# Third decoder layer's cross attention with the keys on the partitions

## The reference

```python
q = x @ Wq                       # [B, 128, 1024]
k, v = jnp.split(context @ Wkv, 2, axis=-1)
sim = einsum('bhid,bhjd->bhij', q, k) * 64 ** (-0.5)
sim = jnp.where(mask, sim, -finfo.max)
sim = jnp.clip(sim, -5.0, 5.0)
attn = jax.nn.softmax(sim, axis=-1)
out = einsum('bhij,bhjd->bhid', attn, v)
return out @ Wo + bo
```

## Time and profile before

| | |
|---|---|
| median of three runs | 2144.5 us |
| profiled execution, span | 2139.6 us |
| PE busy | 1891.7 us, 88% |
| DVE busy | 1520.1 us, 71% |
| ACT busy | 1370.0 us, 64% |
| POOL busy | 827.2 us, 39% |

### The profile page before, as it was taken

One profiled execution on the slowest core, in us unless ns is written; L12 is line 12 of the kernel. 1 busy time (PEld: TensorE's weight loads), 2 busy tenths in 40 slices (PEclk: granted clock), 3 DMA queues, 4 the chain that ended last, 5 costly groups with the idle time before them and its releaser, 6 DMA issues. The chain is left out here.

```text
span 2139.6 us, 40133 instructions
## 1 busy us (share of the span) xinstructions
PE 1891.7 (88%) x13875; PEld 1361.0 (64%) x13945; DVE 1520.1 (71%) x4153; ACT 1370.0 (64%) x5428; POOL 827.2 (39%) x951
## 2 busy tenths in 40 slices
PE   6998989889998998998888999615899996899998
PEld 5757944535786965874444688404467775467776
DVE  4676788788655666779789855695876664786665
ACT  3686589827654587668963765343677774567666
POOL 2461056615432354025643533111543333543334
PEclk9999999979999999999998999867999998999999
DMA  5000000000001000000000000300000000000000
GB/s 228 1 1 1 2 1 1 1 1 2 1 2 34 1 2 1 1 2 1 1 1 1 1 2 1 111 0 13 1 2 1 1 1 24 1 1 1 1 1 11
DMA packets 6980, 24.79 MB, mean 12 GB/s; under 512 B 752, under 2 KB 3440, under 8 KB 6128
## 3 DMA queue, kind: packets, MB, share of 16 engines
q1 hardware_dynamic: 6768, 22.09, 2.8%
HBM read 21.04 MB, written 1.05 MB: 10 GB/s over the span
## 5 line engine op out<-in xcount | busy, mean ns | idle before, releaser
L1358 POOL TENSOR_TENSOR a_probs<-a_probs,a_rinv 128x512 f32<-128x512 f32 x352 | 367.3, 1044 | 421.9 <-DVE a_rinv L1191 417.5
L997 ACT ACTIVATE a_probs<-score_bank,a_negmax 128x128 f32<-128x128 f32 x896 | 315.7, 370 | 64.5 <-DVE a_negmax L1171 62.8
L1358 POOL TENSOR_TENSOR c_probs<-c_probs,c_rinv 128x512 f32<-128x512 f32 x192 | 201.1, 1047 | 296.2 <-DVE c_rinv L1191 294.2
L836 PEld LDWEIGHTS second_bank<-const,a_probs 128*128 128x128 f32 x1408 | 167.4, 142 | 193.4 <-DVE a_probs_t L1198 101.4
L803 PE MATMUL score_bank<-a_km,a_qg 128*128 128x512 f32 x512 | 267.6, 604 | 2.6 <-issue 0.9
L836 PE MATMUL second_bank<-const,a_probs 128*128 128x128 f32 x1408 | 218.4, 278 | 40.8 <-DVE a_probs_t L1198 32.8
L1366 POOL TENSOR_TENSOR a_rstd<-a_ve,neg_half 128x1 f32<-128x1 f32 x128 | 70.5, 551 | 357.6 <-DVE a_ve L1249 356.2
L1171 DVE TENSOR_REDUCE a_negmax<-score_bank 128x4 f32<-128x512 f32 x224 | 154.0, 687 | 67.7 <-PE score_bank L803 53.0
L997 ACT ACTIVATION_READ_ACCUMULATOR a_probs<-score_bank,a_negmax 128x1 f32 x896 | 188.2, 210 | 0.0
L1198 DVE COPY a_probs_t<-second_bank 128x512 f32<-128x512 f32 x272 | 179.6, 660 | 3.9 <-PE second_bank L836 3.9
L1021 ACT ACTIVATE c_probs_t<-second_bank 128x512 f32<-128x512 f32 x160 | 95.3, 595 | 109.9 <-PE second_bank L836 109.5
(11 more groups left out here) (308 smaller groups left out, 4590.3 us busy)
## 6 DMA issues: line engine op xcount, KB each, us to landing
w_L_ffn<-in_L_ffn SPq DMA_DIRECT2D x1, 3184.0 KB, 14.4
w_L_xattn<-in_L_xattn SPq DMA_DIRECT2D x1, 2112.0 KB, 24.2
w_L_xattn<-in_L_xattn SPq DMA_DIRECT2D x1, 2050.0 KB, 10.3
a_xt<-in_xT SPq DMA_DIRECT2D x3, 512.0 KB, 3.6
a_x<-in_x SPq DMA_DIRECT2D x3, 512.0 KB, 3.7
a_ct<-in_ctxT SPq DMA_DIRECT2D x3, 512.0 KB, 5.8
w_L_attn<-in_L_attn SPq DMA_DIRECT2D x1, 1345.5 KB, 17.2
w_L_attn<-in_L_attn SPq DMA_DIRECT2D x1, 1157.0 KB, 5.8
```

Of the source, the lines that this page charges most:

```text
L836: mm = pe.transpose(bank[:, j * S:(j + 1) * S], Pb[:, n % 4, j * S:(j + 1) * S], ident)
L997: op = act.activation(p, score_bank[n % 3][:, j * width:(j + 1) * width], ACT.Exp, bias=negmax[:, n % 4, j:j + 1], accum_out=rsum[:, n % 4 ...
L1358: pool.tensor_tensor(p, p, along(rinv[:, n % 4, 0:heads], 512 // heads), ALU.mult).then_inc(sems["norm_done"], 1)
```

## The change

Scores are computed the other way round, keys on the partitions and queries along the row, so that the values product can take the exponentials as they are and nothing has to be transposed. What follows from it:

- Two units (8 heads) form a pair. The scores of both are issued together, into two score banks: K64 is the stationary operand, the query the moving one, and each product contracts over only the 64 partitions of its head, even heads in partitions 0 to 63 and odd heads in 64 to 127, in turn. Qz with its zeros becomes Qc, without.
- ACT takes the exponential of a whole unit in one instruction (128 x 512, from the score bank), without row sums. POOL then clips the exponentials to between exp(-5) and exp(5), and to exp(-5) for a masked key, whose bound is now one number a partition.
- For a pair PE does 8 value products, from the unnormalised exponentials, and 8 more with a 128 x 64 block of ones as the stationary operand into `second_bank`, which gives each row sum in all 64 partitions of a head.
- DVE takes the reciprocal of `second_bank` (128 x 512) and multiplies `value_bank` by it into OT. ACT's copy L1038, DVE's clip, its small reciprocal and its copy of the transposes go.
- The probability tiles are 6 instead of 4. Qc, K64, V64 share memory with Q8 of the first layer. The mask's DMA is no longer a row of bytes for each partition but one byte for each key and sequence, laid across the partitions (128 x 8 bytes).

```diff
+TURNED = ("mqa", "h64m") + H8
...
-                Qz = sb(tag + "qz", [P, 2, 8, 2, S], scope=scope)
-                K64 = sb(tag + "k64", [P, 2, 8, S], scope=scope)
+                ends = sb(tag + "ends", [P, 6144], scope=scope)
+                Qc = ends[:, 0:2048].rearrange("p (a c k) -> p a c k", a=2, c=8)
...
-                mask_u8 = sb(tag + "mask_u8", [P, G, S], U8, scope=scope)
-                clip_hi = sb(tag + "clip_hi", [P, G, S], scope=scope)
+                mask_u8 = sb(tag + "mask_u8", [P, G], U8, scope=scope)
+                clip_hi = sb(tag + "clip_hi", [P, G], scope=scope)
...
+                    if name == "mask_bk1":
+                        return nc.sync.dma_start(mask_u8[:, :], of.rearrange("a (g p) -> p (a g)", p=P), allow_slow_non_contiguous=True)
...
-                        pool.memset(Qz[0:64, :, :, 1, :], 0.0)
-                        pool.memset(Qz[64:128, :, :, 0, :], 0.0)
+                        pool.memset(ones[:, :], 1.0)
...
                         elif kind == "h64c":
+                            score_bank_free(n + 1)
                             for j in range(4):
-                                mm = pe.matmul(bank[:, j * S:(j + 1) * S], Qz[:, plan.ring(s, 2), 2 * i + j // 2, j % 2, :], K64[:, plan.ring(s, 2), 2 * i + j // 2, :], start=True, stop=True)
+                                for odd in range(2):
+                                    half = slice(64 * odd, 64 * odd + 64)
+                                    mm = pe.matmul(score_bank[(n + odd) % 3][:, j * S:(j + 1) * S], K64[half, plan.ring(s, 2), 2 * i + j, :],
+                                                   Qc[half, plan.ring(s, 2), 2 * i + j, :], start=True, stop=True)
...
                         elif kind == "h64c":
                             for j in range(4):
-                                h = 4 * i + j
-                                mm = pe.matmul(value_bank[64 * (j % 2):64 * (j % 2) + 64, (j // 2) * S:(j // 2 + 1) * S],
-                                               V64[:, plan.ring(s, 2), 0, h * 64:(h + 1) * 64], pt[:, j * S:(j + 1) * S], start=True, stop=True)
+                                for odd in range(2):
+                                    h = 2 * (4 * (i // 2) + j) + odd
+                                    half = slice(64 * odd, 64 * odd + 64)
+                                    p = Pb[:, (n - 1 + odd) % PROBS, j * S:(j + 1) * S]
+                                    pe.matmul(value_bank[half, j * S:(j + 1) * S], V64[:, plan.ring(s, 2), 0, h * 64:(h + 1) * 64], p, start=True, stop=True)
+                            for j in range(4):
+                                for odd in range(2):
+                                    half = slice(64 * odd, 64 * odd + 64)
+                                    mm = pe.matmul(second_bank[half, j * S:(j + 1) * S], ones[:, :], Pb[:, (n - 1 + odd) % PROBS, j * S:(j + 1) * S], start=True, stop=True)
...
+                                act.activation(Pb[:, n % PROBS, :], score_bank[n % 3][:, :], ACT.Exp).then_inc(sems["exp_done"], 1)
...
+                    def divided(n):
+                        s, i, kind, b = plan.unit(n)
+                        if kind != "h64c" or i % 2 == 0:
+                            return
+                        dve.wait_ge(sems["values_ready"], plan.count("values", n))
+                        link(dve.reciprocal(rsums[:, :], second_bank[:, :]))
+                        dve.tensor_tensor(OT[:, plan.ring(s, 2), 4 * (i // 2):4 * (i // 2) + 4, :], heads_view(value_bank[:, :], 4), heads_view(rsums[:, :], 4), ALU.mult).then_inc(sems["out_taken"], 1)
...
+                            p = Pb[:, n % PROBS, :]
+                            pool.tensor_scalar(p, p, CLIP_LOW, clip_hi[:, b:b + 1], ALU.max, ALU.min).then_inc(sems["norm_done"], 1)
```

More of the change, by code:

```diff
@@ L16 @@
+import math
 from contextlib import ExitStack
@@ L62 @@
     "negmax": ("mqa", "h64m") + H8,
-    "moved": ("h64c", "h64m", "h8p"),
+    "moved": ("h64m", "h8p"),
     "exp": SOFTMAX,
+    "sums": TURNED,
     "norm": SOFTMAX,
@@ L195, in count @@
             return sum(self.copier(k) == stage for k in range(n + 1))
+        if stage == "values":
+            return sum(self.kind(s) in SOFTMAX and (self.kind(s) != "h64c" or i % 2) for s, i in self.units[:n + 1])
         return sum(self.kind(s) in STAGES[stage] for s, _ in self.units[:n + 1])
@@ L863, in values @@
                                     after_reader(pe, s, name)
-                        wait_once(pe, sems[stage], plan.count(stage, n))
+                        if kind == "h64c":
+                            if i % 2 == 0:
+                                return
+                            wait_once(pe, sems["norm_done"], plan.count("norm", n))
+                            turned = [k for k in range(n) if plan.unit(k)[2] in TURNED]
+                            wait_once(pe, sems[plan.copier(turned[-1])], plan.count(plan.copier(turned[-1]), turned[-1]))
+                        else:
+                            wait_once(pe, sems[stage], plan.count(stage, n))
                         outs = out_before(n)
@@ L1025, in outs @@
                         s, i, kind, b = plan.unit(n)
-                        if kind in H8 and i < 3 or kind not in SOFTMAX:
+                        if kind in H8 and i < 3 or kind not in TURNED:
                             return
```

79 lines of the change are left out of this document (41 added, 38 removed).

## The result

The changed kernel took 2203.9 us in the median of four runs (2201.3 to 2206.9), the kernel before, run beside it, 2145.4 us. The ratio is 1.028, 95% interval 1.026 to 1.029: slower by 58 us. The forecast was 2187 us, so the sign and the mechanism are the forecast's, and 17 us more were lost than it says. That is inside the range given (2152 to 2218) and above the forecast's own (2178 to 2200).

What follows compares the result with a forecast made beforehand. L2_xattn was taken as bound by PE alone before, by a chain through PE and DVE after. 2139.6 + 38.4 (two turns) + 2 (mask) + 2 (clock) = 2182.0, median 4.9 above: 2187 us, range 2152 to 2218.

Steps and rivals of the forecast that it cites:

- The reciprocal: DVE's 128x512 reciprocal of the row sums: 3.46 us, carried on from narrow rows at 6.47 ns a column; bounds 0.69 to 5.4.
- R: Answer time from a pair's last values-block load on PE to DVE's quotient being ready for PE: 4.52 us.
- the two waits: PE waits for DVE's quotient: about 1.5 us before each second pair's values, about 2.5 us before the output product.
- Half-array scores: Score products on PE: two halves run beside one another, 0.053 us a pass, 0.85 a pair plus 0.17 on each side.
- Rival C: Half-array scores gain nothing beside full ones at full clock: 0.94 us more for each pair outside the waits, 2204 us; chance 0.12.
- The lead: PE's scores, transposes and values for this part ahead of its start at 573.90: 6.2 us becomes 3.6, -2.6 a turn.
- The mask: The mask's DMA, now 1024 runs of one byte, delays the loop's start: +2 us, once.
- ACT and POOL: Both engines' work in this part becomes less and neither bounded anything: no effect on the time.
- PE's clock: Granted clock falling in PE's new waits, at the last pair and output: 1 us a turn, +2 in all.
- The median above the span: The measured median lies 4.9 us above the profiled span, added to 2182.0 to give 2187 us.
- The busy sums: Engines' total busy time: DVE's up by some 35 us, PE's down by some 30.

Runs made afterwards that it cites:

- e_serial: Changed kernel with a pair's eight half-array score products as four of the upper half, then four of the lower, instead of in turn: 2215.7 us, 1.034.
- e_wide: e_first with a pair's row sums by two products of 512 columns, one for each half of the array, instead of eight of 128: 2136.9 us, 0.997.
- e_mult: Changed kernel with POOL's clip replaced by a multiplication of two tensors by the mask's bound, which changes the probabilities: 2205.3 us, 1.029.
- e_warm: Changed kernel with eight products of 128x128, later overwritten, ahead of PE's wait before each output product of this part: 2188.9 us, 1.021.
- e_copy: Changed kernel with the 128x512 reciprocal replaced by a copy of the same shape, so the division by row sums is left out: 2117.7 us, 0.988.
- e_first: e_early with the products with ones also ahead of the scores products of their slot: 2137.6 us, 0.998.
- e_turn: e_pair with a unit's transposes ahead of the next pair's scores within a slot of this part: 2145.3 us, 1.000.
- e_pair: Kernel before with paired half-array scores and paired values products only; clip before the exponential, ACT's row sums, transposes and POOL's division stay: 2134.1 us, 0.996.
- e_early: Changed kernel with row sums and reciprocal one slot ahead of their pair's values, only the multiplication left behind the values: 2155.8 us, 1.007.

## Why the prediction was right, and where it was short

The step that carries the forecast held: a reciprocal without cover stands between PE's products and their readers, and both waits and the period are as derived. Several of its terms were off, and the largest miss is the clock's.

- **The reciprocal, 3.46 us.** Measured 3.36. Carrying on the slope from 36 columns was right; the bounds of 0.69 and 5.4 us were far off. The Trainium skill's repeat count (VectorE: DVE Perf Modes, "First, the fixed hardware budget") was read as 8 cycles a column, an estimate of 4.3 us; here it is 6.4 ns, and the measurement decides.
- **R and the two waits.** The last load of the sums ends at 618.60 and the output product starts at 623.11: 4.51 us, forecast 4.52. The sum is this close by luck: the reciprocal is 0.10 shorter and the last handover, from DVE's end at 622.96 to PE, 0.15 instead of 0.05. The period at full clock was 17.50, forecast 17.37.
- **Half-array scores, 53 ns a pass, 1.19 a pair.** Measured 1.09 with its change of mode. Rival C named 2204 us, the measured time, but its condition (0.11 us a pass) is false, so only the number is C's. The reason given, "two halves run beside one another, at twice the rate", holds (e_serial, e_wide).
- **The lead, -2.6.** From the last v projection ahead of the part (554.93 before, 557.01 after) to the part's start it is 18.97 and 16.92 us: -2.1. But that projection comes 2.1 us later than before, of which the mask accounts for about 1, so the part starts where it did, at 573.93 for 573.90; in the second turn the change gains 1.0 us ahead of the part. Where the rest goes wasn't looked into.
- **The mask, +2.** The sign held; measured 1.0 us in the profiled runs (19.70 for 18.70), 0.3 to 1.2 over all kernels.
- **ACT and POOL, nothing.** Held (e_mult), though POOL's work did not get less: the clip takes 1.99 us where the product took 1.04, and POOL's busy sum rose from 827.2 to 884.9. "The clip must be ready five slots after its scores" was the reason that held.
- **PE's clock, +1 a turn: the step that failed.** The prediction took as its evidence one window of the kernel before that kept 1.00 with waits of about a microsecond, and wrote "I take 1 each". Measured 10.5 and 9.8 us a turn over the sum. Of these e_warm gave back 7.7 (144.1 to 136.3) and 6.2 (143.4 to 137.2) by work without use; of the 2.7 left in the first turn 2.2 lie in the two periods where its clock still fell. Its nearest bound was "3.5 us a turn if the last pair and output ran at 0.50", and it was too narrow. For what it counts it was right: the last pair and output product lost 3.3 us in the first turn. But eight more blocks behind waits of 2.35 to 4.3 us, in the first, sixth and seventh period, took 1.1 to 1.9 times their time. With 20.3 in place of the 2 the sum gives 2182.0 + 18.3 = 2200.3 for the span; 2204.5 was measured. Of the 4.2 left, 1.9 arise behind loop A, where the forecast has nothing, and 2.3 in the lead and the mask taken together.
- **The median above the span, +4.9.** This is chance. The profiled run of the kernel before was the fastest of its three; a run's time is some 1.7 us above its own span (2206.2 and 2204.5 for the changed kernel), and here the median lies below the profiled span. The term made up for part of what the clock lacked.
- **The busy sums.** DVE's rose by 41 us, forecast some 35. PE's fell by 6.5 and not by some 30: in a period at 1.00 it fell from 15.53 to 13.94, but the blocks at a low clock count as busy for longer, by some 18 us.

Why the clock falls behind a wait of 2.35 us in one period and not in the next is open. In the first turn periods two to five have the same waits as the sixth (all 1.20 and 2.35) and kept 1.00; in the second turn it is the third that fell, and the first and the sixth that kept it; in e_mult's first turn the first kept it and the second fell. No run here separates this.

## What to carry over

Price an instruction that is put between a product and its reader by its length on the path, and then ask what can be moved between them: the same reciprocal cost 86 us behind the values (the changed kernel against e_copy) and about 20 ahead of the scores (e_first against e_copy). Move both ends of a handover: PE's order without DVE's (e_turn) bought a longer wait. And where PE goes from busy to waiting two to four microseconds at a time, put a term for the clock into the sum that is as large as the blocks behind the waits, not a token. Here it came to about 10 us a turn for sixteen waits of 1.0 to 4.8 us.

The fastest version with the full arithmetic was e_pair, 2134.1 us; e_first and e_wide, which keep the change's layout, came within 4 us of it, which their intervals don't tell apart from none.

## What the runs showed of the hardware

- Two halves of PE's array, used in turn, ran side by side at both widths measured. Full-array passes take 0.112 us for 128 columns and 0.43 for 512; half-array passes in turn take 0.053 to 0.058 for 128 and, without the change of mode, about 0.21 for 512 (1.01 us for four, less 0.17). Eight passes of one half, then eight of the other, gained next to nothing (0.10 a pass in e_serial). The Trainium skill (TensorEngine Tiling (Array Packing), Key Properties) says that tiles can load and multiply in parallel; for products of 128 and 512 columns this case agrees.
- DVE's reciprocal: 6.4 ns a column from 64 to 512 columns, with 0.09 us on top; a copy of the same 128x512 took 0.69 us.
- POOL's TENSOR_SCALAR on 128x512: 0.62 us for mult and add, 1.57 for a min by partition, 1.93 to 1.99 for max and min.
- The granted clock: in the changed kernel twelve output products stand behind waits of 2.35 or 2.38 us; nine kept their 2.02 us and three took 2.42 to 2.71. Behind each of its eight waits of 3.18 to 4.77 us the block took 1.4 to 1.9 times its time; in e_early an output product behind 3.39 us kept its 2.02 us. A wait of a given length did not decide it by itself.
